# Ten of eleven blocks of a transformer kernel end without GpSimd's drain

## What is computed

```python
x = x + L0_xattn(ctx, norm(x))      # two hops of softmax attention over ctx
x = x + L0_ffn(norm(x))             # 8 experts, top 2, gelu
x = x + L1_xattn(norm(x), ctx)      # linear attention, 16 heads
x = x + L1_ffn(norm(x))             # 8 experts, top 2, gated, capacity
x = x + L2_xattn(ctx, norm(x))      # 16 heads of 64, softmax
x = x + L2_ffn(norm(x))             # 8 experts, top 2, gated
x = x + L3_xattn(norm(x), ctx)      # one head, masked softmax
x = x + L3_ffn(norm(x))             # 8 experts, top 1, gelu
```

## Time and profile before

| what | us |
|---|---|
| median of 3 runs | 1701.94 |
| lowest and highest of them | 1701.4, 1706.82 |
| span of the profiled execution | 1769.0 |
| TensorE busy in that span | 1426.5 |
| VectorE busy | 1112.7 |
| ScalarE busy | 892.0 |
| GpSimd busy | 768.7 |

### The profile page before, as it was taken

One profiled execution on the slowest core, in us unless ns is written; L12 is line 12 of the kernel. 1 busy time (PEld: TensorE's weight loads), 2 busy tenths in 40 slices (PEclk: granted clock), 3 DMA queues, 4 the chain that ended last, 5 costly groups with the idle time before them and its releaser, 6 DMA issues. The chain is left out here.

```text
span 1769.0 us, 37485 instructions
## 1 busy us (share of the span) xinstructions
PE 1426.5 (81%) x10866; PEld 1315.8 (74%) x10867; DVE 1112.7 (63%) x3494; ACT 892.0 (50%) x2683; POOL 768.7 (43%) x764
## 2 busy tenths in 40 slices
PE   6665779975677569999999999999993999366494
PEld 4554579964556459999999999999992888154494
DVE  5634544438766457777777778787875455585343
ACT  4443135541223148777777777777771222243252
POOL 3064424430002545565656565666453455005342
PEclk9886779995576879999999999999997999677697
DMA  9311112213022130000000000000001322601224
GB/s 232 19 37 36 40 50 64 64 47 139 24 95 59 39 97 11 13 1 18 9 17 7 16 7 16 7 4 7 5 9 41 110 70 68 198 1 36 66 63 121
DMA packets 94444, 87.05 MB, mean 49 GB/s; under 512 B 17108, under 2 KB 81079, under 8 KB 93959
## 3 DMA queue, kind: packets, MB, share of 16 engines
q1 hardware_dynamic: 75240, 56.44, 12.1%
q0 software_dynamic: 11936, 24.55, 4.2%
q10 hardware_dynamic: 7168, 4.86, 1.0%
HBM read 54.03 MB, written 33.35 MB: 49 GB/s over the span
## 5 line engine op out<-in xcount | busy, mean ns | idle before, releaser
L2159 POOL TENSOR_TENSOR paired_rows<-paired_rows,rinv 128x1024 f32<-128x1024 f32 x128 | 242.4, 1894 | 245.1 <-DVE rinv L2474 230.3
L2465 DVE TENSOR_TENSOR probs_turned_lo<-psum_banks,probs_turned_hi 128x512 fp32r<-128x512 f32 x256 | 175.7, 686 | 141.9 <-ACT probs_turned_hi L2324 118.8
L2350 ACT ACTIVATE paired_rows<-psum_banks,neg_max 128x256 f32<-128x256 f32 x512 | 236.7, 484 | 1.1 <-DVEq L2051 0.4
L2271 PE MATMUL psum_banks<-probs_turned_hi,y_rows 128*128 128x256 f32 x1024 | 213.8, 292 | 0.9 <-DVEq L2051 0.9
L2221 PE MATMUL psum_banks<-y_turned_parts,queries_hi 128*128 128x256 f32 x1024 | 198.7, 292 | 3.0 <-DVEq L2051 3.0
L2271 PEld LDWEIGHTS psum_banks<-probs_turned_hi,y_rows 128*128 128x128 f32 x1024 | 167.1, 189 | 1.7 <-DVEq L2051 1.5
L2324 ACT CAST probs_turned_hi<-psum_banks 128x512 fp32r<-128x512 f32 x256 | 151.2, 591 | 20.4 <-PE psum_banks L2192 10.5
L2192 PE MATMUL psum_banks<-ident,paired_rows 128*128 128x128 f32 x1024 | 155.9, 275 | 6.9 <-DVE probs_turned_lo L2465 4.5
L2221 PEld LDWEIGHTS psum_banks<-y_turned_parts,queries_hi 128*128 128x128 f32 x1024 | 157.2, 190 | 3.5 <-issue 3.5
L2480 DVE TENSOR_REDUCE neg_max<-psum_banks 128x4 f32<-128x1024 f32 x128 | 155.5, 1215 | 5.5 <-PE psum_banks L2221 3.5
L2221 PE MATMUL psum_banks<-y_turned_parts,queries_lo 128*128 128x256 f32 x512 | 144.3, 282 | 0.0
(11 more groups left out here) (698 smaller groups left out, 3781.4 us busy)
## 6 DMA issues: line engine op xcount, KB each, us to landing
paired_rows<-expert_rows SPq DMA_DIRECT2D x16, 512.0 KB, 6.0
tile_rows<-rows_by_expert SPq DMA_DIRECT2D x110, 64.5 KB
tile_rows<-rows_by_expert_first SPq DMA_DIRECT2D x71, 64.5 KB
expert_w_b<-in_L_ffn_w_dram SPq DMA_DIRECT2D x2, 2048.0 KB, 12.9
tile_rows<-expert_rows SPq DMA_DIRECT2D x8, 512.0 KB
x_rows<-in_x_dram SPq DMA_DIRECT2D x8, 256.0 KB, 5.2
ctx_turned_dram<-ctx_turned SPq DMA_DIRECT2D x1, 2048.0 KB, 10.4
normed_rows_dram<-paired_rows SPq DMA_DIRECT2D x1, 2048.0 KB, 8.7
```

The lines of the kernel that those rows point to most:

```text
L2159: ins = pool.tensor_tensor(probs[:, k, :, :], probs[:, k, :, :], rinv[:, k, :].unsqueeze(2).to_broadcast([P, 4, 256]), ALU.mult)
L2271: ins = pe.matmul(bank[Z_BANK][:, r * 256:(r + 1) * 256], yrows[:, 2 * s1 + y, (2 * r + k) * P:(2 * r + k + 1) * P], probsT[x][:, (u + 1) ...
L2350: ins = act.activation(probs[:, par, h, :], bank[S_BANKS[par] + h // 2][:, (h % 2) * 256:(h % 2 + 1) * 256], ACT.Exp, bias=nmax[:, par, h: ...
L2465: ins = dve.tensor_tensor(lo, bank[bank_][:, :], hi.bitcast(F32), ALU.subtract)
```

## The change

The seven places that open a block, all but the one in combine_and_store, pass `no_gpsimd_drain=True`. As experts is called four times, ten of the eleven blocks are changed. Such a block ends with a drain on each of the four other engines and then a barrier that consists of semaphore instructions only; GpSimd runs no DRAIN at its end. The last block keeps the form with GpSimd's drain. Nothing else is changed, and each of the seven edits has this form:

```diff
-            block = ph.enter_context(nc.Block())
+            block = ph.enter_context(nc.Block(no_gpsimd_drain=True))
```

## The result

| | median, us | runs | ratio to the kernel before | 95% interval |
|---|---|---|---|---|
| kernel before | 1701.94 | 7 | | |
| changed kernel | 1692.47 | 7 | 0.9938 | 0.9918 to 0.9959 |

The changed kernel is 0.6% faster: by the ratio 10.5 us, with an interval of 7.0 to 14.0. The ratio is not the quotient of the two medians, which lie 9.5 us apart. Measured twice more on other occasions, the ratio was 0.9941 and 0.9935. The forecast was 1694.8 us, 7.1 us under the median before.

The account below looks back on a forecast made before the run. The prediction took what ends last at ten barriers as the bound, GpSimd's DRAIN at the four experts ends. Terms: -17.6 + 0.6 + 9.9 = -7.1 us, from 1701.9 to 1694.8 us; range 1687 to 1703.

Parts of the forecast that it names:

- Four DRAINs on the path, -17.6: Ends of the four experts calls: GpSimd's DRAINs of 5.85, 2.67, 5.85 and 3.23 us go, -17.6 us.
- Drains off the path, 0: attention_0 to attention_3, route(1), first block: something else ends these blocks, so removing their drains gains 0.
- Barrier, +0.06 a block: End of each of ten blocks: the new barrier form costs +0.06 us, together +0.6 us (-1 to +2).
- 82 ns for each open DMA: Any GpSimd drain: some 82 ns for each indirect DMA issued and not yet accounted for.
- L2088, 13.7 us: GpSimd's first drain in attention_2: finds 167 open DMAs and takes 13.7 us, where it now takes 0.25.
- the prediction's own sign for the first rival: In the profile: L2088's first DRAIN near 9 to 10 us, with slower issues in experts(1).
- the first rival: List of open DMAs limited between 71 and 167, middle 119: L2088 exposes 6.0 us, total 1692.2 us; chance 0.27.
- the same estimate: From the skill's pages: 113 DMAs fit the list, L2088 takes 9.3 us, total 1691.7 us.
- Cover 3.8 us, so +9.9 exposed: Start of attention_2: ScalarE's roots wait for VectorE anyway, hiding 3.8 us of L2088's 13.7; +9.9 us exposed.
- The rival's +1.3 in experts(1): Back-to-back issues in experts(1): a limited list adds up to 2.6 us, half taken, +1.3; chance 0.27.
- the slower rival: experts(1), experts(3), attention_3: a full list stalls issues; at 0.6 us a DMA, 1714 us; chance 0.09.
- Last block, 13.0 us, hidden: Last block's kept drain: finds 158 open DMAs, takes 13.0 us, hidden in 18.1 us with 5.1 us of cover.

Follow-up runs that it names:

- e3: Changed kernel with GpSimd's drain kept at the four ends of experts, so taken out only at the six other blocks: 1707.85 us, ratio 1.0038.
- e2: Kernel before with GpSimd's drain taken out only at the four ends of experts, kept at the seven other blocks: 1683.81 us, ratio 0.9919.

## Why the prediction was right, and where it wasn't

- *Four DRAINs on the path, -17.6.* Measured -17.75. Right, and the experts' half alone keeps all of it.
- *Drains off the path, 0.* Right in the sum: nothing was gained by taking them out. The six blocks alone lose time (e3), which is the moved accounting.
- *Barrier, +0.06 a block.* Measured +0.07 where another engine ends the block. Right.
- *82 ns for each open DMA, paid by the next drain of whatever kind.* Right at each of 32, 71, 87 and 103, and whether the drain was a block's or written out.
- *L2088, 13.7 us.* Over-sized; 9.34 measured. The step that failed is the one where I took the upper end because no row showed a DMA being accounted for outside a drain. None could: no stretch of before had more than 71 open, and the freeing begins with the 114th. Of the prediction's own sign for the first rival one half came, a drain "near 9 to 10"; the "slower issues in experts(1)" did not. The Trainium skill's figures, from which the prediction had estimated 113 ("SBUF — State Buffer", section "SBUF size: 192, 224, or 256?", and "DMA: Bandwidth & Descriptors", sections "Terms" and "The descriptor swizzle"), agree with this trace to the DMA: the 114th is the late one. The page's nine descriptors are for a transfer of 1 MiB; the DMAs here move some 64 KB. That the same estimate had L2088 at 9.3 us is luck: 113 x 82 ns is a list that stays full. The list stood at 63 after the 114th and had filled up again to 111 by L2088, with 53 more issued. Why it isn't 116 stays open.
- *Cover 3.8 us, so +9.9 exposed.* The cover was right: 3.8 us at the roots. 5.9 us were exposed, 5.3 from the shorter drain and 0.6 that the sum had no term for, VectorE's L443 and L445 running beside GpSimd's moved work.
- *The rival's +1.3 in experts(1).* Measured 0: the issues there are 1.27 us apart, before and after. The freed half of the list leaves room, so the price isn't paid one by one. That also does away with the slower rival: a full list cost 0.84 us once in experts(0) and 0.40 + 0.30 in attention_3, and the next work hid both (attention_3's tail is 4.08 us before and after).
- *Last block, 13.0 us, hidden.* Measured 6.4, hidden. The count was wrong for the same reason, and it didn't matter.

With the measured terms the sum is -17.75 + 5.9 + 0.4 (six blocks that another engine ends) = -11.4 us. The three measurements give -10.5, -10.0 and -11.1. The forecast of -7.1 was 3.4 us too careful against the first of them, and the term at L2088, +9.9 in place of +5.9, is more than all of that. The time came out where the first rival had it (1692.2 us), and its +6.0 at L2088 was nearly right, though it had taken the middle between 71 and 167 for the limit.

One choice of method was lucky. I took the terms unscaled from a profile 67 us above the median. The DRAINs repeat to some ns, so that did no harm here. The covers don't repeat: attention_3's looked like 5.3 us and was 1.3, which cost e2 4.6 us where 0.5 was expected.

## What to carry to other kernels

A GpSimd drain pays for every indirect DMA that GpSimd has issued since its last one: 82 ns each here, for up to 103 of them; from the 114th on a part goes without a drain. All of them move 128 rows, some 64 KB, so no run shows whether the price goes by the DMA or by its rows. Taking a drain out saves this only if a later one pays at a place where GpSimd is idle. So count the open DMAs at each drain that stays, and write one drain into an idle stretch before the first drain that something waits for: one such line took the exposed 5.9 us down to 0.8 (0.992 of the time before), and two took the kernel from 0.994 to 0.989. Read covers from a profile whose span is near the median.

## What the hardware did that I had not expected

- A full list isn't kept full. At the 114th open DMA some 51 entries (experts(0)) or 70 (attention_3) go for a delay of 0.84 or 0.40 us against the undisturbed issues, where a drain pays 82 ns for each. In experts(0) GpSimd had been waiting for VectorE there, so the freeing may have taken up to 2.32 us; in attention_3 the issues stand back to back, and 0.40 us for 70 is 6 ns each (10 ns for 72 if the second late issue, 0.30 us, is counted in). The freeing inside an issue is far cheaper than a drain.
- VectorE's operation that adds the pairs (L2537, two operands from SBUF) takes 2.35 us while GpSimd only drains (changed kernel, each time) and 3.02 in the kernel before, where GpSimd computes beside part of it. With the shorter drain of the kernel with two it takes 3.45. The changed kernel, then the one with two drains:

```profile
575.29 2.35 DVE L2537 SCALAR_TENSOR_TENSOR x_rows<-tile_rows,mix_weights,x_rows 128x128 f32<-128x128 f32 x8 [3.04 <-DMA tile_rows<-expert_rows]
```
```profile
567.18 3.45 DVE L2538 SCALAR_TENSOR_TENSOR x_rows<-tile_rows,mix_weights,x_rows 128x128 f32<-128x128 f32 x8 [3.02 <-DMA tile_rows<-expert_rows]
...
572.14 0.56 DVE L2543 TENSOR_SCALAR rows_work<-rows_mv 128x8 f32<-128x8 f32 x1
```

  L2543 also took 0.56 us there against 0.17 for L2542 in the changed kernel. These two are the 0.8 us that attention_2's start still costs with 32 DMAs open: 3.45 - 3.02 + 0.56 - 0.17 = 0.82 us, and ScalarE's roots, which wait for L2543, start 9.05 us after the table load in place of 8.27. The 2.6 us of drain shift GpSimd's work onto VectorE's. Of the eight operations of L2538 the third takes 1.12 us in place of 0.34 and ends 0.14 us after GpSimd's, and L2543 ends 0.03 us after GpSimd's L2084. No run moved GpSimd's work alone, so the cause is read from this coincidence. The Trainium skill has a rule for it ("SBUF — State Buffer", section "Summary: rules for kernel authors"): when VectorE's operation has two inputs in SBUF and GpSimd's reads SBUF, the second of them waits for the first. The trace agrees for L2537, and for L443 and L445 above. L2543 reads one tile only, which the rule in this form doesn't name.
